# First attention of a fused four-layer kernel: sums over two groups at a time, and two projections split around a turn

## The chip, the cores and the metric

The kernel runs on one core of a Trainium2 chip, as one program. The metric is the device time of that core in microseconds, the median of several runs. Lower is better.

## What is computed

Two layers of a gated model, each an attention over a context followed by a feed-forward part, on 16 sequences of 112 tokens by 512 and a context of 375 tokens by 512. The change lies in the first attention alone:

```python
def _mha(q, k, v):                       # q = layernorm(x), k = v = ctx
    scores = jnp.einsum('bhqd,bhkd->bhqk', qh, kh) / math.sqrt(hd)   # 16 heads of 32
    scores = jnp.where(causal[None, None], scores, MASKED_BIAS)
    attn = jax.nn.softmax(scores, axis=-1)
    out = jnp.einsum('bhqk,bhkd->bhqd', attn, vh)
x = x + jnp.tanh(g_xattn[0]) * _L0_xattn_ref(_layernorm(x), ctx, ctx)
...
k = rms_norm((ctx @ Wk).reshape(B, S_enc, 4, 128))   # of the second attention
v = (ctx @ Wv).reshape(B, S_enc, 4, 128)
```

The phase of the first attention also computes the keys and values of the second attention, since it holds the transposed context, and turns and rotates weights and the first outputs for the feed-forward part that follows.

## The kernel before

`phase_a` works through 16 batches, each a sequence. A batch has 16 heads, taken as 8 pairs (n = 0 to 7) and as 4 groups of 4 heads (g = 0 to 3, pairs 2g and 2g+1). Each engine has its own hand-written program; they meet at semaphores, and each engine does its instructions in order. Nothing is scheduled by a planner: the order on TensorE is the sequence of `if n == ...` lines in the loop at the end of `phase_a`, and the loops of the other engines match it.

What TensorE does for a pair:

- at even n, `scores`: the scores of the next group of four heads (12 matmuls, line 910), which use 32 of the array's rows each;
- `turn_probs(b, n, 0)` (line 962): three transposes of the first head's probabilities into the PSUM bank `turned`. ScalarE copies them to `pT` (`probs_copy`, line 543). Then `turn_probs(b, n, 1)` does the second head into the same bank, so it waits for that copy (`pT_first`). VectorE copies the second (line 714), and the first turn of the next pair waits for it (`pT_second`);
- between the two turns and behind the second stands other work, to cover the copies. `weigh(b, g)` (line 972) is the weighted sum of group g: 12 matmuls of 32 columns of the array each, over three parts of the context, into the bank `outp`; the trace counts two matmuls and two weight loads for each. It stands between the turns of pairs 2, 4 and 6 (groups 0, 1 and 2) and of pair 0 of the next batch (group 3). ScalarE copies its block to `oT` (`copy_out`, line 570);
- `project` (line 939) makes keys or values of the second attention: 12 matmuls for each of three parts of the context, in two halves of 6. The other items are transposes of the context (`turn_ctx`, 889), the queries (896), the keys (`turn_keys`, 948), the output (`turn_back`, 980), weight jobs (989 to 1001), and from the third batch on the first output for the feed-forward part (`turn_z`, 1007, and `rotate_z`, 1014).

`outp` is one bank that many items use in turn. The list `out_uses` holds the order of its uses, and `free_out` waits for whoever reads the use before.

ScalarE at pair n: the copy of the first turn, `copy_out`, on some pairs `ctx_hi` or `rotated_hi` (line 593), then the exponentials of pair n+2 (line 535), then copies such as `values_out` (line 557) and `keys_out` (line 566). VectorE at pair n: at even n `maximum` of pair n+2 (lines 705 and 708), `scale_keys` (line 723) or `rotated_lo` (line 755), then the copy of the second turn, then at even n `maximum` of pair n+3. `scale_keys` waits for GpSimd's power (line 452). `turn_ctx(b + 1, 2)`, behind the first turn of pair 3, waits for `values_out(b, 0)`, because it writes the same bank.

`probs` has 4 slots of a pair each, `pT` two slots of a group each. The sync queue loads the context of batch b+2 (`load_ctx`) once `out_ready` says that the batch which held that buffer has been summed.

```python
                    if n in (2, 4, 6) and cur:
                        weigh(b, n // 2 - 1)
                    ...
                    if n == 2 and cur:
                        project(b, "v", 0, 1)
                    ...
                    if n == 6 and cur:
                        project(b, "k", 2, 1)
```

Of the kernel before, what the change touches and what calls it, by code (L numbers as in the profile page):

```python
# [30 lines left out]
HD = D // H  # L31
G = 4
# [86 lines left out]
CTX = 3  # L119
# [30 lines left out]
def phase_a(nc, keep, io, ab):  # L150
# [12 lines left out]
    RING = 4  # L163
# [3 lines left out]
    with Memory(nc, "a") as m:  # L167
# [10 lines left out]
        pT = m.sb("pT", [KP, 2, KC, HPG, S])  # L178
# [96 lines left out]
        def _(sp):  # L275
            def load_ctx(b):
# [9 lines left out]
                if b >= CTX:  # L286
                    sp.wait_ge(out_ready, G * (b - CTX) + G)
# [87 lines left out]
            def load_lead(c):  # L375

                sp.wait_ge(out_ready, G * (B - CTX + c) + G)
# [133 lines left out]
        def _(act):  # L511
# [16 lines left out]
            def exps(b, n):  # L528
# [4 lines left out]
                for i in range(2):  # L533
                    h = 2 * n + i
                    last = act.activation(probs[:, n % RING, i, 0:T], score[0:S, h % HPG, 0:T], ACT.Exp, bias=nmax[:, b % 2, h:h + 1],  # L535
                                          accum_out=sums[:, b % 2, h:h + 1])
                last.then_inc(probs_ready, 1)

            def probs_copy(b, n):

                act.wait_ge(turned_ready, 2 * (PAIRS * b + n) + 1)
                g, half = n // 2, n % 2
                act.activation(pT[:, g % 2, :, 2 * half, :], turned[0:KP, 0:KC * S].rearrange("p (c s) -> p c s", c=KC),  # L543
# [125 lines left out]
        def _(dve):  # L669
# [40 lines left out]
            def probs_copy(b, n):  # L710

                dve.wait_ge(turned_ready, 2 * (PAIRS * b + n) + 2)
                g, half = n // 2, n % 2
                dve.tensor_copy(pT[:, g % 2, :, 2 * half + 1, :], turned[0:KP, 0:KC * S].rearrange("p (c s) -> p c s", c=KC)).then_inc(pT_second, 1)
# [133 lines left out]
        def _(pe):  # L848
# [4 lines left out]
            def free_out(*use):  # L853
# [5 lines left out]
                if kind == "weigh":  # L859
                    pe.wait_ge(out_copied, G * b + i + 1)  # L860
# [53 lines left out]
            def project(b, what, c, half):  # L914
                bank, ready = (keys, k_ready) if what == "k" else (values, v_ready)
                cols = slice(0, D) if what == "k" else slice(D, 2 * D)
                if half == 0:
# [15 lines left out]
                for n, (s, r, k) in enumerate(passes):  # L933
                    if n // 6 == half:
# [6 lines left out]
                if half:  # L941
# [1778 lines left out]
```

## Time and profile before

| | |
|---|---|
| median of 3 runs | 2031.68 us (2031.16 to 2034.02) |
| the profiled execution, its own time | 2032.41 us |
| its span in the trace | 2030.7 us |
| mean granted clock of TensorE | 0.988 of 2.4 GHz |
| TensorE busy | 1964.1 us, 97% |
| its weight loads | 1629.0 us, 80% |
| VectorE, ScalarE, GpSimd busy | 61%, 57%, 42% |

The phase that the change touches is the first 585 us or so of the span. Times are from the start of the span. A row of the time line gives the start, the duration, the engine, the line, the operation, its output and inputs, the shape and how many were merged into the row; in brackets stands how long the engine was idle before it and what ended that. PE is TensorE's matmuls, PEld its weight loads, which run ahead of the matmuls. Matmuls are pipelined: one starts before the one before it has ended, so what a step costs is read from start to start, not from the durations.

### The profile page before, as it was taken

Reading aid. Unit: us, or ns where it says so; the run is one execution under the profiler, and the core shown is the slowest. Engines: PE = TensorE matmul, PEld = TensorE weight load, DVE = VectorE, ACT = ScalarE, POOL = GpSimd, SP = SyncE. Lnnn points to the kernel's source line nnn. Section 1 sums busy time; section 2 is a strip of 40 time slices with the busy share of each in tenths; the row PEclk is TensorE's granted clock in tenths of the full one; section 3 lists DMA queues with packets and bytes.
Section 4 is the critical chain, followed back from the end, with each engine's and each line's share of the span. In section 5 each row is a group of like instructions: output and inputs, shape, how many; then the busy total and the mean of one; then the engine's idle time right before and its main releaser. Section 6 shows DMA issues by size and latency. Waiting matters only on the chain. (4 is left out here: it accounts for less than half of the span.)

```text
span 2030.7 us, 37414 instructions
## 1 busy us (share of the span) xinstructions
PE 1964.1 (97%) x13369; PEld 1629.0 (80%) x13369; DVE 1237.1 (61%) x2272; ACT 1158.6 (57%) x3064; POOL 850.5 (42%) x1010
## 2 busy tenths in 40 slices
PE   7999999999999999999989997899999999989997
PEld 6777777777778888898868886799999999877875
DVE  7767666676645643564445555666666666466665
ACT  6666666666643333453333435877777777354554
POOL 3525536445434000000003444888888888122222
PEclk9999999999999999999999998999999999999999
DMA  5426346344364210203003335333333342421101
GB/s 188 158 95 194 127 129 214 120 160 138 109 224 170 88 63 1 73 1 120 1 26 104 117 113 160 92 86 115 111 102 100 108 117 87 125 64 51 33 29 38
DMA packets 195370, 210.67 MB, mean 104 GB/s; under 512 B 60912, under 2 KB 135712, under 8 KB 194688
## 3 DMA queue, kind: packets, MB, share of 16 engines
q1 hardware_dynamic: 195200, 208.43, 32.6%
q8 instruction: 104, 1.70, 0.4%
q14 instruction: 66, 0.54, 0.1%
HBM read 128.43 MB, written 79.95 MB: 103 GB/s over the span
## 5 line engine op out<-in xcount | busy, mean ns | idle before, releaser
L1883 POOL TENSOR_TENSOR qd_rows<-qd_rows,c_rsum 112x375 f32<-112x375 f32 x256 | 202.5, 812 | 79.1 <-DVE c_rsum L2013 72.7
L2019 DVE TENSOR_TENSOR c_pT_lo<-c_turned,c_pT_hi 128x336 fp32r<-128x336 f32 x256 | 128.4, 502 | 123.6 <-ACT c_pT_hi L1958 123.6
L1949 ACT ACTIVATE qd_rows<-c_score,c_nmax 112x375 f32<-112x375 f32 x256 | 146.9, 574 | 86.8 <-DVE c_nmax L2008 86.8
L1314 ACT ACTIVATE b_silu<-b_gate,ab_scales 128x512 f32<-128x512 f32 (+1 forms) x64 | 40.7, 637 | 253.8 <-PE b_up L1443 253.8
L1380 DVE SCALAR_TENSOR_TENSOR b_hidden<-b_up,ab_scales,b_silu 128x512 f32<-128x512 f32 (+1 forms) x64 | 43.7, 683 | 196.3 <-ACT b_silu L1314 196.3
L2313 POOL TENSOR_TENSOR f_probs<-f_probs,f_rsum 112x448 f32<-112x448 f32 x64 | 59.7, 933 | 206.6 <-DVE f_rsum L2437 206.6
L535 ACT ACTIVATE a_probs<-a_score,a_nmax 112x375 f32<-112x375 f32 x256 | 144.5, 575 | 3.0 <-DVE a_nmax L708 2.9
L2008 DVE TENSOR_REDUCE c_nmax<-c_score 112x1 f32<-112x375 f32 x256 | 137.7, 538 | 0.4 <-PE c_score L2090 0.4
L2352 ACT ACTIVATE f_probs<-f_score,f_nmax 112x112 f32<-112x112 f32 x256 | 86.5, 364 | 80.7 <-DVE f_nmax L2432 80.7
L1292 POOL TENSOR_TENSOR ab_zT<-ab_zT,keep_ln_eps 128x1 f32<-128x1 f32 x1 | 0.2, 190 | 298.7 <-DVE ab_zT L1414 298.7
L962 PE MATMUL a_turned<-keep_ident,a_probs 112*128 112x112 f32 x768 | 122.1, 268 | 1.9 <-ACT a_pT L543 1.0
L708 DVE TENSOR_REDUCE a_nmax<-a_score 112x2 f32<-112x750 f32 x128 | 120.1, 938 | 4.4
L962 PEld LDWEIGHTS a_turned<-keep_ident,a_probs 112*128 112x128 f32 x768 | 86.6, 142 | 40.0 <-issue 23.5
L1958 ACT ACTIVATE c_pT_hi<-c_turned 128x336 fp32r<-128x336 f32 x256 | 100.5, 445 | 26.7 <-PE c_turned L2101 26.7
L2101 PE MATMUL c_turned<-keep_ident,qd_rows 112*128 112x112 f32 x768 | 96.8, 260 | 10.9 <-DVE c_pT_lo L2019 8.6
L2101 PEld LDWEIGHTS c_turned<-keep_ident,qd_rows 112*128 112x128 f32 x768 | 84.9, 141 | 27.9 <-POOL qd_rows L1883 12.0
L705 DVE COPY_PREDICATED a_score<-keep_later,a_score 112x224 f32<-112x224 uint8 x128 | 49.9, 390 | 91.0 <-PE a_score L910 91.0
L2090 PE MATMUL c_score<-c_k_hi,c_q_hi 128*112 128x376 f32 x256 | 95.4, 373 | 5.7 <-DVE c_k_lo L2003 4.8
L1616 ACT ACTIVATE qd_rows<-q_q_bank 128x512 f32<-128x512 f32 x56 | 33.5, 598 | 114.0 <-PE q_q_bank L1725 114.0
L543 ACT ACTIVATE a_pT<-a_turned 128x336 f32<-128x336 f32 x128 | 57.6, 450 | 63.4 <-PE a_turned L962 62.3
L450 POOL TENSOR_TENSOR a_ssq_eps<-a_ssq,keep_rms_eps 128x4 f32<-128x4 f32 x48 | 9.6, 200 | 198.1 <-DVE a_ssq L718 198.1
L1457 PE MATMUL b_y<-b_wd_hi,b_hT_hi 128*128 128x512 f32 x224 | 87.6, 391 | 0.2 <-DVE b_hT_lo L1389 0.2
(354 smaller groups left out, 6025.8 us busy)
## 6 DMA issues: line engine op xcount, KB each, us to landing
q<-q_qT SPq DMA_DIRECT2D x14, 1024.0 KB, 5.7
qd_raws<-q SPq DMA_DIRECT2D x64, 224.0 KB, 3.0
v<-bq_raw SPq DMA_DIRECT2D x48, 256.0 KB, 2.1
qd_raws<-v SPq DMA_DIRECT2D x64, 192.0 KB, 2.8
k<-bq_raw SPq DMA_DIRECT2D x16, 752.0 KB, 4.0
qd_raws<-k SPq DMA_DIRECT2D x64, 188.0 KB, 2.4
wug<-a_ug_turned SPq DMA_DIRECT2D x32, 256.0 KB, 2.2
bq_raw<-in_ctx_dram SPq DMA_DIRECT2D x15, 512.0 KB
```

The costliest lines, as they stand in the source:

```text
L535: last = act.activation(probs[:, n % RING, i, 0:T], score[0:S, h % HPG, 0:T], ACT.Exp, bias=nmax[:, b % 2, h:h + 1], accum_out=sums[:, b % ...
L708: dve.tensor_reduce(nmax[:, b % 2, 2 * n:2 * n + 2], score[0:S, pair, 0:T], axis=AX.X, op=ALU.max, negate=True).then_inc(max_done, 1)
L962: last = pe.transpose(turned[0:KP, c * S:(c + 1) * S], probs[:, n % RING, i, c * KP:(c + 1) * KP], ident[0:S, 0:S])
L1457: last = pe.matmul(y[b][:, :], hT[s][:, p, b * P:(b + 1) * P], wd[r][:, p, :], start=c == 0 and k == 0, stop=c == IC - 1 and k == len(PASS ...
L1883: pool.tensor_tensor(probs[:, n % AHEAD, 0:T], probs[:, n % AHEAD, 0:T], rsum[:, n % (2 * H):n % (2 * H) + 1].broadcast_to([S, T]), ALU.mu ...
L1949: act.activation(probs[:, n % AHEAD, 0:T], score[n % AHEAD][0:S, 0:T], ACT.Exp, bias=nmax[:, c:c + 1], accum_out=sums[:, c:c + 1]).then_in ...
L1958: act.activation(pT[0][:, t % 2, :, j, :], src, ACT.Copy).then_inc(pT_hi, 1)
L2008: dve.tensor_reduce(nmax[:, c:c + 1], score[n % AHEAD][0:S, 0:T], axis=AX.X, op=ALU.max, negate=True).then_inc(max_done, 1)
L2019: dve.tensor_tensor(pT[1][:, t % 2, :, j, :], src, f32(pT[0][:, t % 2, :, j, :]), ALU.subtract).then_inc(pT_split, 1)
L2090: last = pe.matmul(score[n % AHEAD][0:S, 0:TE], q[s][:, t % RING, j, :], k[r][:, t % RING, :], start=i == 0, stop=i == len(PASSES) - 1)
L2101: last = pe.transpose(turned[n % 2][0:KP, c * S:(c + 1) * S], probs[:, n % AHEAD, c * KP:(c + 1) * KP], ident[0:S, 0:S])
L2352: last = act.activation(probs[:, t % RING, j, :], score[0:S, j, columns_of(t)], ACT.Exp, bias=nmax[:, t // 2 % 2, 2 * j + t % 2:2 * j + t ...
```

## The change

The weighted sums are done for two groups at a visit, 24 matmuls into two blocks of `outp`: groups 0 and 1 between the turns of pair 4, groups 2 and 3 between the turns of pair 0 of the next batch. Between the turns of pairs 2 and 6 stand now the first three of the six projection matmuls that used to follow the second turn; the other three follow it as before. ScalarE's copy takes both blocks, 224 columns, so two copies a batch in place of four. `pT` has three slots of a group, so that the groups of a visit stay until it is done; `probs` has three slots of a pair in place of four. The waits and the order of uses of `outp` follow.

```diff
-    RING = 4
+    RING, PT_RING, HALVES = 3, 3, G // 2
-        pT = m.sb("pT", [KP, 2, KC, HPG, S])
+        pT = m.sb("pT", [KP, PT_RING, KC, HPG, S])
...
-            out_uses += [("weigh", b - 1, G - 1), ("keys", b - 1, KC - 1), ("back", b - 1, 0)] if before else []
-            out_uses += [("job", b, 1), ("weigh", b, 0)] if cur else []
+            out_uses += [("weigh", b - 1, HALVES - 1), ("keys", b - 1, KC - 1), ("back", b - 1, 0)] if before else []
+            out_uses += [("job", b, 1)] if cur else []
             out_uses += [("ctx", b + 1, 1)] if after else []
-            out_uses += [("keys", b, 0), ("job", b, 3), ("weigh", b, 1)] if cur else []
+            out_uses += [("keys", b, 0), ("job", b, 3), ("weigh", b, 0)] if cur else []
...
-            out_uses += [("job", b, 5), ("weigh", b, 2), ("keys", b, 1), ("job", b, 7)] if cur else []
+            out_uses += [("job", b, 5), ("keys", b, 1), ("job", b, 7)] if cur else []
...
-                    sp.wait_ge(out_ready, G * (b - CTX) + G)
+                    sp.wait_ge(out_ready, HALVES * (b - CTX) + HALVES)
...
-            def copy_out(b, g):
-                act.wait_ge(out_ready, G * b + g + 1)
-                act.activation(oT[:, g, :], outp[:, 0:S], ACT.Copy).then_inc(out_copied, 1)
+            def copy_out(b, m):
+                act.wait_ge(out_ready, HALVES * b + m + 1)
+                act.activation(oT[:, 2 * m:2 * m + 2, :], outp[:, 0:2 * S].rearrange("p (g s) -> p g s", g=2), ACT.Copy).then_inc(out_copied, 1)
...
-                        copy_out(b - 1, G - 1)
-                    if n in (2, 4, 6) and cur:
-                        copy_out(b, n // 2 - 1)
+                        copy_out(b - 1, HALVES - 1)
+                    if n == 4 and cur:
+                        copy_out(b, 0)
...
-            def project(b, what, c, half):
+            def project(b, what, c, first, end):
...
-                    if n // 6 == half:
+                    if first <= n < end:
...
-            def weigh(b, g):
-                pe.wait_ge(pT_first, PAIRS * b + 2 * g + 2)
-                pe.wait_ge(pT_second, PAIRS * b + 2 * g + 2)
-                free_out("weigh", b, g)
-                for c in range(KC):
-                    for j in range(HPG):
-                        h = HPG * g + j
-                        last = pe.matmul(outp[rows(j), 0:S], ctx[:, b % CTX, c, h * HD:(h + 1) * HD], pT[:, g % 2, c, j, :],
-                                         start=c == 0, stop=c == KC - 1)
+            def weigh(b, m):
+
+                pe.wait_ge(pT_first, PAIRS * b + 4 * m + 4)
+                pe.wait_ge(pT_second, PAIRS * b + 4 * m + 4)
+                free_out("weigh", b, m)
+                for i in range(2):
+                    g = 2 * m + i
+                    for c in range(KC):
+                        for j in range(HPG):
+                            h = HPG * g + j
+                            last = pe.matmul(outp[rows(j), i * S:(i + 1) * S], ctx[:, b % CTX, c, h * HD:(h + 1) * HD],
+                                             pT[:, (G * b + g) % PT_RING, c, j, :], start=c == 0, stop=c == KC - 1)
                 last.then_inc(out_ready, 1)
...
-                        weigh(b - 1, G - 1)
+                        weigh(b - 1, HALVES - 1)
...
-                    if n in (2, 4, 6) and cur:
-                        weigh(b, n // 2 - 1)
+                    if n == 2 and cur:
+                        project(b, "v", 0, 6, 9)
+                    if n == 4 and cur:
+                        weigh(b, 0)
+                    if n == 6 and cur:
+                        project(b, "k", 2, 6, 9)
...
                     if n == 2 and cur:
-                        project(b, "v", 0, 1)
+                        project(b, "v", 0, 9, 12)
...
                     if n == 6 and cur:
-                        project(b, "k", 2, 1)
+                        project(b, "k", 2, 9, 12)
```

TensorE's order at pair 2 of a batch in the middle, from the first turn on, before (a_outp<-a_pT is weigh, a_values is the projection, a_outp<-keep_ident,bq_raw is turn_ctx of part 1, the last row turn_ctx of part 2):

```order
L962 MATMUL a_turned<-keep_ident,a_probs 128x112 x3
L972 MATMUL a_outp<-a_pT,bq_raw 32x112 x12
L962 MATMUL a_turned<-keep_ident,a_probs 128x112 x3
L939 MATMUL a_values<-a_w_lo,a_kT_hi 128x512 x2
L939 MATMUL a_values<-a_w_hi,a_kT_lo 128x512 x4
L889 MATMUL a_outp<-keep_ident,bq_raw 128x128 x4
L962 MATMUL a_turned<-keep_ident,a_probs 128x112 x3
L889 MATMUL a_values<-keep_ident,bq_raw 128x128 x4
```

and now:

```order
L962 MATMUL a_turned<-keep_ident,a_probs 128x112 x3
L939 MATMUL a_values<-a_w_lo,a_kT_hi 128x512 x2
L939 MATMUL a_values<-a_w_hi,a_kT_lo 128x512
L962 MATMUL a_turned<-keep_ident,a_probs 128x112 x3
L939 MATMUL a_values<-a_w_hi,a_kT_lo 128x512 x3
L889 MATMUL a_outp<-keep_ident,bq_raw 128x128 x4
L962 MATMUL a_turned<-keep_ident,a_probs 128x112 x3
L889 MATMUL a_values<-keep_ident,bq_raw 128x128 x4
```

The 12 matmuls of weigh are gone from between the two turns, and three of the six projection matmuls stand there.

TensorE's order at pair 6 of the same batch, before (a_values<-ab_zT is rotate_z, a_keys the projection, a_outp<-keep_ident,a_kn is turn_keys of part 1, and the last row but one is the first turn of pair 7):

```order
L962 MATMUL a_turned<-keep_ident,a_probs 128x112 x3
L972 MATMUL a_outp<-a_pT,bq_raw 32x112 x12
L1014 MATMUL a_values<-ab_zT,keep_hadamard 128x448
L962 MATMUL a_turned<-keep_ident,a_probs 128x112 x3
L939 MATMUL a_keys<-a_w_lo,a_kT_hi 128x512 x2
L939 MATMUL a_keys<-a_w_hi,a_kT_lo 128x512 x4
L948 MATMUL a_outp<-keep_ident,a_kn 128x128 x4
L962 MATMUL a_turned<-keep_ident,a_probs 128x112 x3
```

and now:

```order
L962 MATMUL a_turned<-keep_ident,a_probs 128x112 x3
L939 MATMUL a_keys<-a_w_lo,a_kT_hi 128x512 x2
L939 MATMUL a_keys<-a_w_hi,a_kT_lo 128x512
L1017 MATMUL a_values<-ab_zT,keep_hadamard 128x448
L962 MATMUL a_turned<-keep_ident,a_probs 128x112 x3
L939 MATMUL a_keys<-a_w_hi,a_kT_lo 128x512 x3
L948 MATMUL a_outp<-keep_ident,a_kn 128x128 x4
L962 MATMUL a_turned<-keep_ident,a_probs 128x112 x3
```

Again three projection matmuls take the place of weigh; rotate_z stays between the turns, behind them.

TensorE's order at pair 4, before (a_outp<-keep_ident,a_xn is the transposes of the queries):

```order
L962 MATMUL a_turned<-keep_ident,a_probs 128x112 x3
L972 MATMUL a_outp<-a_pT,bq_raw 32x112 x12
L962 MATMUL a_turned<-keep_ident,a_probs 128x112 x3
L939 MATMUL a_values<-a_w_hi,a_kT_hi 128x512 x4
L939 MATMUL a_values<-a_w_lo,a_kT_hi 128x512 x2
L896 MATMUL a_outp<-keep_ident,a_xn 128x112 x4
```

and now:

```order
L962 MATMUL a_turned<-keep_ident,a_probs 128x112 x3
L975 MATMUL a_outp<-a_pT,bq_raw 32x112 x24
L962 MATMUL a_turned<-keep_ident,a_probs 128x112 x3
L939 MATMUL a_values<-a_w_hi,a_kT_hi 128x512 x4
L939 MATMUL a_values<-a_w_lo,a_kT_hi 128x512 x2
L896 MATMUL a_outp<-keep_ident,a_xn 128x112 x4
```

The visit has 24 matmuls in place of 12. At pair 0 it grows in the same way.

## Rows read from the trace of the kernel before

**Rows 1.** 40 to 560 us: length, then busy us of PE, PEld, DVE, ACT, POOL, PEclk, DMA.

```profile
40.00:560.00 520.00, 519.20 (x4653) 403.26 (x4651) 354.93 (x629) 351.73 (x928) 250.40 (x274) 1.00 0.44 143
```

**Rows 2.** Time line: TensorE at pair 2 of batch 8; start, duration, then what it is.

```profile
308.32 0.51 PE L962 MATMUL a_turned<-keep_ident,a_probs 112*128 112x112 f32 x3
...
308.75 0.54 PEld L972 LDWEIGHTS a_outp<-a_pT,bq_raw 128*32 128x32 f32 x24
...
309.47 0.51 PE L962 MATMUL a_turned<-keep_ident,a_probs 112*128 112x112 f32 x3
...
309.74 0.71 PE L939 MATMUL a_values<-a_w_lo,a_kT_hi 128*128 128x512 f32 x2
...
310.29 1.09 PE L939 MATMUL a_values<-a_w_hi,a_kT_lo 128*128 128x512 f32 x4
...
311.22 0.60 PE L889 MATMUL a_outp<-keep_ident,bq_raw 128*128 128x128 f32 x4
...
311.65 0.45 PE L962 MATMUL a_turned<-keep_ident,a_probs 112*128 112x112 f32 x3
...
312.16 0.63 PE L889 MATMUL a_values<-keep_ident,bq_raw 128*128 128x128 f32 x4
```

**Rows 3.** Time line: ScalarE and VectorE at the same pair 2.

```profile
308.86 0.45 ACT L543 ACTIVATE a_pT<-a_turned 128x336 f32<-128x336 f32 x1 [1.94 <-PE a_turned L962]
...
310.03 0.69 DVE L723 TENSOR_TENSOR a_kn<-a_keys,a_rk 128x512 f32<-128x512 f32 x1 [0.22 <-POOL a_rk L452]
...
310.64 0.50 DVE L714 COPY a_pT<-a_turned 128x336 f32<-128x336 f32 x1
310.86 0.20 ACT L535 ACTIVATION_READ_ACCUMULATOR a_probs<-a_score,a_nmax 112x1 f32 x1
...
311.42 0.60 ACT L557 ACTIVATE bq_raw<-a_values 128x512 f32<-128x512 f32 x1 [0.36 <-PE a_values L939]
```

**Rows 4.** Time line: TensorE at pair 6 of batch 8.

```profile
325.69 0.51 PE L962 MATMUL a_turned<-keep_ident,a_probs 112*128 112x112 f32 x3
...
326.84 1.02 PE L1014 MATMUL a_values<-ab_zT,keep_hadamard 128*128 128x448 f32 x2
...
327.69 0.45 PE L962 MATMUL a_turned<-keep_ident,a_probs 112*128 112x112 f32 x3
...
327.92 0.71 PE L939 MATMUL a_keys<-a_w_lo,a_kT_hi 128*128 128x512 f32 x2
...
329.82 0.45 PE L962 MATMUL a_turned<-keep_ident,a_probs 112*128 112x112 f32 x3
```

**Rows 5.** Time line: ScalarE and VectorE at the same pair 6.

```profile
327.89 0.55 ACT L593 ACTIVATE ab_xr_hi<-a_values 128x448 fp32r<-128x448 f32 x1 [0.66 <-PE a_values L1014]
...
328.47 0.62 DVE L755 SCALAR_TENSOR_TENSOR ab_xr_lo<-a_values,ab_xr_hi 128x448 fp32r<-128x448 f32 x1 [1.29 <-ACT ab_xr_hi L593]
...
329.01 0.50 DVE L714 COPY a_pT<-a_turned 128x336 f32<-128x336 f32 x1
```

**Rows 6.** Time line: pair 6 of batch 1, which has no rotation.

```profile
78.57 0.51 PE L962 MATMUL a_turned<-keep_ident,a_probs 112*128 112x112 f32 x3
...
80.27 0.51 DVE L714 COPY a_pT<-a_turned 128x336 f32<-128x336 f32 x1 [0.21 <-PE a_turned L962]
```

**Rows 7.** Groups by line and form: weigh's weight loads, and the copy of its block.

```profile
L972 PEld LDWEIGHTS a_outp<-a_pT,bq_raw 128*32 128x32 f32 x1536 | 34.6, 109 | 9.8 <-issue 1.0
...
L570 ACT ACTIVATE a_oT<-a_outp 128x112 f32<-128x112 f32 x64 | 16.8, 263 | 18.9 <-PE a_outp L972 18.7
```

**Rows 8.** Time line: TensorE at pair 0 of batch 9, weigh and turn_keys.

```profile
334.89 0.78 PE L972 MATMUL a_outp<-a_pT,bq_raw 128*32 128x112 f32 x24
...
336.38 0.60 PE L948 MATMUL a_outp<-keep_ident,a_kn 128*128 128x128 f32 x4
```

**Rows 9.** Time line: a turn of pair 7, batch 15, released by ScalarE's copy.

```profile
577.07 0.44 ACT L543 ACTIVATE a_pT<-a_turned 128x336 f32<-128x336 f32 x1
...
577.57 0.51 PE L962 MATMUL a_turned<-keep_ident,a_probs 112*128 112x112 f32 x3 [0.37 <-ACT a_pT L543]
```

More of the change, by code:

```diff
@@ L534, in exps @@
                     h = 2 * n + i
-                    last = act.activation(probs[:, n % RING, i, 0:T], score[0:S, h % HPG, 0:T], ACT.Exp, bias=nmax[:, b % 2, h:h + 1],
+                    last = act.activation(probs[:, t % RING, i, 0:T], score[0:S, h % HPG, 0:T], ACT.Exp, bias=nmax[:, b % 2, h:h + 1],
                                           accum_out=sums[:, b % 2, h:h + 1])
@@ L541, in probs_copy @@
                 act.wait_ge(turned_ready, 2 * (PAIRS * b + n) + 1)
-                g, half = n // 2, n % 2
-                act.activation(pT[:, g % 2, :, 2 * half, :], turned[0:KP, 0:KC * S].rearrange("p (c s) -> p c s", c=KC),
+                k, half = divmod(PAIRS * b + n, 2)
+                act.activation(pT[:, k % PT_RING, :, 2 * half, :], turned[0:KP, 0:KC * S].rearrange("p (c s) -> p c s", c=KC),
                                ACT.Copy).then_inc(pT_first, 1)
@@ L712, in probs_copy @@
                 dve.wait_ge(turned_ready, 2 * (PAIRS * b + n) + 2)
-                g, half = n // 2, n % 2
-                dve.tensor_copy(pT[:, g % 2, :, 2 * half + 1, :], turned[0:KP, 0:KC * S].rearrange("p (c s) -> p c s", c=KC)).then_inc(pT_second, 1)
+                k, half = divmod(PAIRS * b + n, 2)
+                dve.tensor_copy(pT[:, k % PT_RING, :, 2 * half + 1, :], turned[0:KP, 0:KC * S].rearrange("p (c s) -> p c s", c=KC)).then_inc(pT_second, 1)
             def sum_keys(b, c):
@@ L912, in scores @@
                 last.then_inc(scores_ready, 1)
-            def project(b, what, c, half):
+            def project(b, what, c, first, end):
                 bank, ready = (keys, k_ready) if what == "k" else (values, v_ready)
                 cols = slice(0, D) if what == "k" else slice(D, 2 * D)
-                if half == 0:
+                if first == 0:
                     if what == "v" and c == 2 and b >= 2:
@@ L940, in project @@
                                          start=n == 0, stop=n == len(passes) - 1)
-                if half:
+                if end == len(passes):
                     last.then_inc(ready, 1)
@@ L961, in turn_probs @@
                 for c in range(KC):
-                    last = pe.transpose(turned[0:KP, c * S:(c + 1) * S], probs[:, n % RING, i, c * KP:(c + 1) * KP], ident[0:S, 0:S])
+                    last = pe.transpose(turned[0:KP, c * S:(c + 1) * S], probs[:, t % RING, i, c * KP:(c + 1) * KP], ident[0:S, 0:S])
                 last.then_inc(turned_ready, 1)
-            def weigh(b, g):
-                pe.wait_ge(pT_first, PAIRS * b + 2 * g + 2)
-                pe.wait_ge(pT_second, PAIRS * b + 2 * g + 2)
-                free_out("weigh", b, g)
-                for c in range(KC):
-                    for j in range(HPG):
-                        h = HPG * g + j
-                        last = pe.matmul(outp[rows(j), 0:S], ctx[:, b % CTX, c, h * HD:(h + 1) * HD], pT[:, g % 2, c, j, :],
-                                         start=c == 0, stop=c == KC - 1)
+            def weigh(b, m):
[9 more added lines that the diff above has]
+                                             pT[:, (G * b + g) % PT_RING, c, j, :], start=c == 0, stop=c == KC - 1)
                 last.then_inc(out_ready, 1)
             def turn_back(b):
-                pe.wait_ge(out_copied, G * b + G)
+                pe.wait_ge(out_copied, HALVES * b + HALVES)
                 free_out("back", b, 0)
@@ L1019, in _ @@
             scores(0, 0)
-            project(0, "k", 0, 0)
+            project(0, "k", 0, 0, 6)
             for b in range(B + 1):
@@ L1086, in _ @@
                         run_job(b, 7)
-                        project(b, "v", 2, 1)
+                        project(b, "v", 2, 6, 12)
 IC = INTER // P
```

22 lines of the change are left out of this document (11 added, 11 removed).

## The prediction

> **What bounds the kernel now.** I read the summary page first: TensorE is busy for 97% of the span. The table of stretches then shows that in the middle of the first attention, from 40 to 560 us, it is busy for 519.20 of 520 us at a granted clock of 1.00, while VectorE and ScalarE are at 355 and 352 us [rows 1]. The view of waits lists no wait of TensorE's matmuls there. So in this phase TensorE's own chain of starts is the time, and an edit is worth what it changes between two starts on TensorE. The other engines matter only where a release comes later than TensorE would arrive. I therefore read the time line around the two pairs that change, in one batch; the 16 batches repeat it within 0.02 us, but for the first two and the last.
>
> I count from T, the start of the first turn of a pair. Pair 2 of batch 8 has T = 308.32 [rows 2]: weigh starts at T+0.43, the second turn at T+1.15, the projection (6 matmuls) at T+1.42, turn_ctx at T+2.90, pair 3's first turn at T+3.33 and its turn_ctx at T+3.84. Pair 6 has T = 325.69 [rows 4]: rotate_z at T+1.15, the second turn at T+2.00, pair 7's first turn at T+4.13.
>
> **What a visit costs.** From weigh's start to the next is 0.72 us, and reaching it takes 0.43 after T, against 0.27 for a projection behind a turn (309.47 to 309.74) [rows 2]. A visit issues 24 weight loads of 109 ns [rows 7], and all 24 lie within 0.54 us [rows 2]: (0.54 - 0.11)/23 = 0.0187 us from one to the next. Twelve more matmuls, thus 24 more loads in the same mode, cost 24 x 0.0187 = 0.45 us. This length isn't in the trace of before. Its bounds are 0.45 (the rate of the row goes on) and 0.72 (the second group pays a whole visit). I take 0.45, since nothing stands between the groups and the operands have the same shape. The Trainium skill speaks against it: "TensorE: Matmul & The Clock Gate", part 3 on packing small matmuls, says that a weight load overlaps running matmuls only where the row group differs, and these loads fill all rows. By that rule the 24 loads would be serial, 24 x 0.109 = 2.6 us in place of 0.45. The row shows them overlapped, so I keep 0.45.
>
> **Added:** pairs 4 and 0 get the longer visit: 16 + 16 visits x 0.45 = **+14.4 us**. It lies on TensorE's chain, with nothing beside it. The last of these, behind the last batch, delays the end of the phase by the same 0.45.
>
> **Removed at pair 2 (16 times).** If TensorE were never held up: three projection matmuls start at T+0.27; two take 0.55 (309.74 to 310.29) and one 0.23 (a quarter of 310.29 to 311.22), so the second turn would be at T+1.05. It waits for ScalarE's copy, which ends at T+0.99 [rows 3]; with a release of 0.06 to 0.14 (below) that is T+1.05 to T+1.13, a loss under 0.1 that what follows hides. Then 0.23 to the projection (327.69 to 327.92 [rows 4]), 0.78 for three matmuls (the first behind a turn is dearer), 0.43 for turn_ctx: pair 3 would begin at T+2.49, 0.84 earlier than now. **Two releases don't allow that.** VectorE copies pair 2's second probabilities behind maximum and scale_keys. scale_keys starts at T+1.71, where GpSimd's a_rk releases it, and the copy ends at T+2.82 [rows 3]. All of that hangs on work of pair 1 or on the scores, which start no earlier relative to T, so it stays. And turn_ctx of part 2 waits for values_out: ScalarE ends its exponentials at T+2.74, needs 0.60 for the copy, so it can end at T+3.37 (now T+3.70) [rows 3]. A release takes 0.14 us from the end of the copy to the start of the matmul where two conditions are waited for (312.02 to 312.16) [rows 2, 3] and 0.06 where there is one (577.51 to 577.57) [rows 9]. I take 0.14, as both places have two. So pair 3 begins at T+2.96 and its turn_ctx at T+3.51, against T+3.84: a gain of 0.33, x 16 = **-5.3 us**.
>
> **Removed at pair 6.** Without holds: rotate_z at T+0.27+0.78 = T+1.05, second turn 0.85 later, then 0.23 + 0.78 + 0.44, so pair 7 at T+3.35. But its first turn waits for a chain that begins at rotate_z: ScalarE's rotated_hi (T+2.20), VectorE's rotated_lo (T+2.78), then its copy of the probabilities, which ends at T+3.82 [rows 5]. rotate_z comes only 0.10 earlier, so the copy ends at T+3.72 and pair 7 begins at T+3.86 to T+3.87, against T+4.13: a gain of 0.26 where 0.78 were there to take; x 13 (batches 2 to 14) = **-3.4 us**. The first two batches have no rotation: their copy ends at T+2.21 [rows 6], ahead of need at T+2.49, and I give them pair 2's free gain of 0.84 to 0.85. The last batch computes no keys for a next one and has slack around this pair; I give it the same: 3 x 0.85 = **-2.6 us**.
>
> **Costed at nothing.** The block's copy grows from 112 to 224 columns: 263 ns now [rows 7], 450 for 336 columns [rows 3], so about 0.36 by line. At pair 0 it must end before turn_keys(2), which starts 1.49 us behind weigh now [rows 8] and 1.94 in the new order; the block is ready at 0.78 + 0.45 = 1.23, its copy at some 1.66, released by 1.80. The cover is 0.14 us; if it is gone, each 0.1 us lost costs 1.6 us. RING of 3 adds no wait: the slot asked for was turned before the copy that precedes the exponentials on ScalarE. The third pT buffer is written behind a turn that itself stands behind the visit that read it. On the sync queue, load_ctx and what is queued behind it go at most 0.45 later; its data are due a batch later. DVE's and POOL's orders are unchanged.
>
> **Sum:** +14.4 - 5.3 - 3.4 - 2.6 = **+3.1 us**. The profiled execution took 2032.41 us (span 2030.7), 0.73 above the median of the three runs, so it becomes 2035.5 and the median 2031.68 becomes **2034.8 us**. One measurement of this kernel tells 0.2% from no change, which is 4.06 us: 2027.6 to 2035.7. My number is inside, near the upper edge.
>
> **Rivals.**
> *A, the holds are not there, faster.* If VectorE's and ScalarE's chains move forward with TensorE, the gains are 16 x 0.84 + 13 x 0.78 + 3 x 0.85 = 26.1 us against 14.4: -11.7, thus 2020.0. For it: both engines idle almost a third of the phase. Against it: the rows put the two copies at T+2.82 and T+3.82, behind work that starts from T. Chance 0.09.
> *B, the second group isn't free of entry and exit, slower.* The mechanism is in weigh itself: if the array empties between the two groups, as between a turn and a visit, the visit grows by 0.72 and not by 0.45: 32 x 0.27 = 8.6 more, +11.7, thus 2043.4. It would decide from 0.03 us more a visit (0.9/32), since my sum is 0.9 below the edge. For it: every change of kind around weigh costs 0.16 to 0.18 us. Against it: inside a visit three accumulations of four matmuls follow each other with no gap in the loads. Chance 0.10.
> *C, serial weight loads.* If loads that fill all rows couldn't overlap, the second group would cost 2.6 us: 32 x (2.6 - 0.45) = 69 more, thus 2104. The row of 24 loads in 0.54 us speaks against it. Chance 0.01. This is the rule of the Trainium skill's TensorE page, part 3, quoted above.
>
> **How the numbers follow.** The forecast has the remaining 0.80. Its own bounds: with releases of 0.06 the two gains grow by 0.08 each, 29 x 0.08 = 2.3 lower, 2032.5; a reading error of 0.03 us at each of 61 places is 1.8 either way, a loss of 0.1 at the tight copy of pair 0 adds 1.6, and the first two batches and the last, taken by analogy, are good for 1.7 either way. That is 2029 to 2040, the range, with A, B and C outside (0.20). Of the 0.80, 0.02 lie below 2027.6, 0.50 within 0.2%, and 0.28 above 2035.7. So faster 0.09 + 0.02 = 0.11, same 0.50, slower 0.28 + 0.10 + 0.01 = 0.39.
>
> **What would show it.** In the profile after: weigh with 48 loads in about 1.0 us, and 1.16 to 1.17 to the next start; pair 2's first turn to pair 3's first turn 2.96 us, with a wait on pT of VectorE of some 0.4 us, 16 times; pair 6 to pair 7 3.87 us with such a wait of 0.5 us, 13 times; a batch longer by 0.9 - 0.33 - 0.26 = 0.3 us. I am wrong if VectorE's copy stops being the release of these turns (A), if the loads show a gap between the 24th and the 25th (B), or if turn_keys at pair 0 begins to wait for the block's copy.

## The result, and the profile after

The changed kernel's median is 2033.67 us over 20 runs (2031.34 to 2037.84), that of the kernel before beside it 2031.54 us over 20 runs. The ratio is 1.0013, with a 95% interval from 1.0007 to 1.0019: slower by 2.6 us (1.4 to 3.9), which is clear of zero and within the 0.2% that I called no change. The forecast was 3.1 us more. The profiled execution took 2032.96 us, its span is 2031.2.

The stretch of [rows 1], for the kernel after (the columns are length, then busy us of PE, PEld, DVE, ACT, POOL, PEclk, DMA share, GB/s):

```profile
40.00:560.00 520.00, 511.39 (x4606) 397.29 (x4604) 352.04 (x625) 339.96 (x889) 247.99 (x272) 1.00 0.44 143
```

TensorE is no longer busy all the time, 511.39 us of 520 against 519.20. What took the rest is named by the view of waits, 40 to 560 us, matmuls of TensorE (total us, times, longest):

```profile
PE a_turned L962 <- ACT a_probs L535: 4.6, 13, 0.4
PE a_turned L962 <- DVE a_pT L714: 3.6, 14, 0.3
```

The kernel before had no row here. There are now 27 waits: at pair 3 in 14 batches and at pair 7 in 13, those in the window. The name ACT a_probs on the second kind is misleading: the turn waits for two conditions, and the view names the one whose signal it saw last. The experiment on pair 6 shows that it is VectorE's copy: with that copy earlier, the turn starts at T+3.26 while the same ScalarE row still runs to T+3.67. No other wait of TensorE's matmuls stands in this view, so the ring of three slots, the third buffer of `pT` and the later loads of the context, which the prediction put at nothing, held no matmul here.

Pair 2 of batch 8 in the time line, answering [rows 2, 3]:

```profile
308.11 0.51 PE L962 MATMUL a_turned<-keep_ident,a_probs 112*128 112x112 f32 x3
...
310.42 0.50 DVE L714 COPY a_pT<-a_turned 128x336 f32<-128x336 f32 x1
310.65 0.20 ACT L535 ACTIVATION_READ_ACCUMULATOR a_probs<-a_score,a_nmax 112x1 f32 x1
310.74 0.60 ACT L557 ACTIVATE bq_raw<-a_values 128x512 f32<-128x512 f32 x1
...
311.07 0.48 PE L962 MATMUL a_turned<-keep_ident,a_probs 112*128 112x112 f32 x3 [0.26 <-DVE a_pT L714]
...
311.48 0.63 PE L889 MATMUL a_values<-keep_ident,bq_raw 128*128 128x128 f32 x4
```

With T = 308.11 VectorE's copy ends at T+2.81, pair 3 begins at T+2.96 and its turn_ctx at T+3.37 (before: T+2.82, T+3.33, T+3.84). The second turn starts at 309.16, T+1.05. Those but the last are the forecast to 0.01 us; turn_ctx is 0.14 earlier than forecast.

Pair 6 of batch 8, answering [rows 4, 5]:

```profile
325.57 0.51 PE L962 MATMUL a_turned<-keep_ident,a_probs 112*128 112x112 f32 x3
...
326.63 0.91 PE L1017 MATMUL a_values<-ab_zT,keep_hadamard 128*128 128x448 f32 x2
...
327.58 0.54 ACT L593 ACTIVATE ab_xr_hi<-a_values 128x448 fp32r<-128x448 f32 x1 [1.01 <-PE a_values L1017]
...
328.16 0.62 DVE L755 SCALAR_TENSOR_TENSOR ab_xr_lo<-a_values,ab_xr_hi 128x448 fp32r<-128x448 f32 x1 [1.10 <-ACT ab_xr_hi L593]
...
328.70 0.50 DVE L714 COPY a_pT<-a_turned 128x336 f32<-128x336 f32 x1
...
329.34 0.48 PE L962 MATMUL a_turned<-keep_ident,a_probs 112*128 112x112 f32 x3 [0.36 <-ACT a_probs L535]
```

With T = 325.57: rotate_z at T+1.06, rotated_hi T+2.01, rotated_lo T+2.59, VectorE's copy ends T+3.63, pair 7 begins T+3.77 (before T+4.13, forecast T+3.86). rotate_z behind a projection takes 0.75 us to the next start, not the 0.85 that it took behind weigh, and the chain moves forward by that.

The visit, at pair 4 of batch 8, with its weight loads:

```profile
316.69 0.51 PE L962 MATMUL a_turned<-keep_ident,a_probs 112*128 112x112 f32 x3
...
317.13 1.12 PEld L975 LDWEIGHTS a_outp<-a_pT,bq_raw 128*32 128x32 f32 x48
...
318.42 0.51 PE L962 MATMUL a_turned<-keep_ident,a_probs 112*128 112x112 f32 x3
```

From weigh to the next start it is 1.29 us, not the 1.17 of the forecast. The reason is in the rate. The stretches count every load that overlaps a slice of 0.1 us; a load lasts 0.11, so it counts about twice. Before (batch 8, pair 2), loads of line 972 alone:

```profile
308.80:308.90 0.10, 0.10 (x12) 1.00 0.85 307
...
309.00:309.10 0.10, 0.10 (x9) 1.00 0.78 287
```

After (pair 4), loads of line 975:

```profile
317.20:317.30 0.10, 0.10 (x12) 1.00 0.00 0
317.30:317.40 0.10, 0.10 (x8) 1.00 0.00 0
...
318.00:318.10 0.10, 0.10 (x8) 1.00 0.94 369
```

The first eight come close together (12 in a slice), then it is 8 in every slice. By the starts of the single loads in the trace, the first eight lie within 0.05 us and from then on four follow every 0.096 us, in both kernels: 0.024 us a load. The 25th starts 0.077 us behind the 24th, as the first of every four does, so there is no gap between the two groups. My 0.0187 was the mean over a visit that had the dense beginning in it. Twelve more matmuls, 24 loads, cost 24 x 0.024 = 0.58 us. The matmuls keep the same step, four every 0.096 us, so the trace doesn't say whether the loads or the matmuls set it.

The block's copy took 357 ns for 224 columns (forecast 0.36), by the groups of lines.

Batch 8 to batch 9, from pair 2's first turn to the next pair 2's, is 35.25 us after (308.11 to 343.36) and was 34.95: +0.30 a batch, with +0.31 forecast. (Some batches take longer, up to 35.8 us before; from the third on each grows by 0.3 to 0.4.)

**Why the two spans differ by 0.5 us only.** The spans are 2030.7 and 2031.2, and yet the phase has grown by more. The profiled executions start differently. The stretch from 17 to 27 us, of the kernel before, of the kernel after, and of the kernel after in another execution (the first experiment below):

```profile
17.00:27.00 10.00, 8.48 (x44) 6.41 (x40) 8.25 (x14) 6.17 (x15) 0.41 (x2) 0.66 0.85 261
```

```profile
17.00:27.00 10.00, 7.78 (x54) 5.74 (x55) 9.16 (x16) 5.97 (x16) 1.88 (x4) 1.00 0.86 253
```

```profile
17.00:27.00 10.00, 8.16 (x52) 6.30 (x49) 8.36 (x15) 5.86 (x15) 1.14 (x4) 0.83 0.86 262
```

The granted clock (the number before the last two) is 0.66, 1.00 and 0.83 of 2.4 GHz there, the last two for the same code: where the mean is under 1.00, TensorE ran at the lower level, 1.2 GHz, for part of the stretch. In all three it had waited before, for the first copies of the probabilities (0.58 us at 18 us, 0.9 to 1.3 us at 20 us); the execution that stayed at 1.00 waited no less, so what decides stays open. The kernel before reached pair 2 of batch 0 at 27.52 us, the one after at 25.49: 2.0 us that are no work of the change. From there to the first matmul of the next phase it is 558.41 and 562.01 us (which starts at 585.93 and 587.50). So in these two executions the phase grew by 3.6 us, and in the other execution of the kernel after it is 562.05 us again. The remaining 1.0 us lies behind the phase, whose code is the same: 1444.8 us before, 1443.7 after, and 1442.1 in the other execution of the kernel after. The timed runs give 1.4 to 3.9 for the change.

### The profile page after: what moved, and what is told of

Read it like the earlier page. It is cut to its first block and busy times, and to the rows that moved or that the text cites. A ratio compares the mean times of both kernels' runs of the same rounds, so it can differ in the third digit from the quotient of the medians.

```text
span 2031.2 us, 37351 instructions
## 1 busy us (share of the span) xinstructions
PE 1958.2 (96%) x13369; PEld 1624.6 (80%) x13369; DVE 1236.8 (61%) x2272; ACT 1149.7 (57%) x3032; POOL 850.6 (42%) x1010
## 5 line engine op out<-in xcount | busy, mean ns | idle before, releaser
L962 PEld LDWEIGHTS a_turned<-keep_ident,a_probs 112*128 112x128 f32 x768 | 84.4, 141 | 56.6 <-issue 27.5
L2131 PE MATMUL c_y<-o_wo_hi,c_oT_lo 128*128 128x512 f32 x224 | 87.7, 391 | 0.0
```

The source lines that it names most:

```text
L962: last = pe.transpose(turned[0:KP, c * S:(c + 1) * S], probs[:, t % RING, i, c * KP:(c + 1) * KP], ident[0:S, 0:S])
L2131: last = pe.matmul(y[:, :], oT[s][:, h, place], wo[r][:, h, :], start=h == 0 and n == 0, stop=h == H - 1 and n == len(PASSES) - 1)
```

## Experiments

Nine other kernels ran after the prediction, and the changed one once more, in three groups, each on a chip of its own beside the kernel before. Ratios are to that kernel, with their 95% intervals; between groups the ratios are compared, not the medians. Numbers behind T are from their traces, batch 8 unless said.

The traces give a second measure, which leaves out the start and everything behind the phase: from pair 2 of batch 0 to the first matmul of the next phase. The two executions of the changed kernel agree in it to 0.03 us, while the rest of the span, behind the phase, lies anywhere from 1442.1 to 1447.4 us in the twelve profiled executions. For each kernel, what differs from the kernel before (558.41 us in this measure; in brackets the name that the quoted expectations use):

| kernel | phase, by its trace | timed runs (from the ratio) |
|---|---|---|
| the change | +3.6 us | +2.6 us (+1.4 to +3.9) |
| the change once more | +3.6 | +2.6 (+0.8 to +4.5) |
| pair 6 (a_dve6) | -3.1 | -5.9 (-8.1 to -3.7) |
| pair 2 (a_dve2) | +3.5 | +2.8 (+1.0 to +4.5) |
| pair 2 again (a_dve2_pe3) | +2.9 | +1.6 (-0.2 to +3.5) |
| both (a_all) | -4.4 | -4.5 (-6.5 to -2.4) |
| both, and context part 2 later (a_all2) | -11.6 | -12.4 (-15.2 to -9.5) |
| the five moves in the kernel before | -3.5 | -3.0 (-4.9 to -1.2) |
| VectorE's two orders in the kernel before | +0.2 | +1.6 (-0.2 to +3.5) |
| visits issued twice | +36.7 | +36.2 (+33.1 to +39.0) |
| projections whole again | +3.9 | +4.1 (+1.8 to +6.3) |

The two measures agree within the intervals, but for pair 6, where the trace gives 0.6 us less than the edge; why isn't shown.

### The changed kernel once more

No edit.

> The changed kernel itself, beside the others on this chip: 0.07 to 0.19% above the kernel before, a batch 0.30 us longer in its trace. If instead it is level or faster, the slower result was the chip's and not the kernel's.

Measured: 1.0013 (1.0004 to 1.0022), median 2033.62. The result stands in a second measurement.

### Pair 6: VectorE's copy ahead of rotated_lo

```diff
-                    if n == 6 and b >= 2 and cur:
-                        rotated_lo(b - 2)
                     if n == 7 and cur:
                         sum_keys(b, 2)
                     if cur:
                         probs_copy(b, n)
+                    if n == 6 and b >= 2 and cur:
+                        rotated_lo(b - 2)
```

> The changed kernel, with VectorE's copy of pair 6's probabilities ahead of rotated_lo. Theory (VectorE's copy, queued behind rotated_lo, holds pair 7's first turn): the copy ends at T+2.8, so that turn comes at T+3.35 in place of T+3.77, in 13 batches: 5.5 us less than the changed kernel, about 2028.2, which is 0.16% below the kernel before. The projection of pair 7 waits for rotated_lo, due at T+3.57 as before, so no new wait. Rival (another release stands right behind, for instance rotated_lo itself for that projection): nothing gained, 2033.7.

Measured: 0.9971 (0.9960 to 0.9982), median 2025.98. Against the changed kernel's 1.0013 that is 0.42% or 8.5 us less; the batch went from 35.25 to 34.73 us (306.38 to 341.11), which over 13 batches is 6.8; the phase is 6.7 us shorter in its trace. The forecast of 5.5 was too low, and the 8.5 of the timed runs has room for 6.7 in its interval. Its pair 6:

```profile
323.83 0.51 PE L962 MATMUL a_turned<-keep_ident,a_probs 112*128 112x112 f32 x3
...
326.13 0.51 DVE L714 COPY a_pT<-a_turned 128x336 f32<-128x336 f32 x1 [0.81 <-PE a_turned L962]
...
326.55 0.61 DVE L755 SCALAR_TENSOR_TENSOR ab_xr_lo<-a_values,ab_xr_hi 128x448 fp32r<-128x448 f32 x1
...
327.09 0.45 PE L962 MATMUL a_turned<-keep_ident,a_probs 112*128 112x112 f32 x3
```

The copy ends at T+2.81 and pair 7 begins at T+3.26, with no wait. The next row of the chain, rotated_lo, ends at T+3.33 and held nobody. So the wait was VectorE's copy behind rotated_lo, and moving one line of one queue turns the change from slower into faster than the kernel before. The expected T+3.35 was 0.09 too late, for the shorter rotate_z.

### Pair 2: VectorE's copy ahead of scale_keys

```diff
-                    if n == 2 and cur:
-                        scale_keys(b, 0)
...
                     if cur:
                         probs_copy(b, n)
+                    if n == 2 and cur:
+                        scale_keys(b, 0)
```

> The changed kernel, with VectorE's copy of pair 2's probabilities ahead of scale_keys. Theory (two releases hold pair 3, and the later one is ScalarE's values_out for turn_ctx): pair 3's first turn moves from T+2.96 to T+2.50, but turn_ctx of part 2 stays at T+3.37, so the time stays within 1 us of 2033.7. Rival (VectorE's copy alone is the hold): 16 x 0.46 = 7.4 us less, 2026.3.

Measured: 1.0014 (1.0005 to 1.0022), median 2033.54, as the changed kernel; the phase is 0.1 us shorter. Its pair 2:

```profile
309.13 0.51 PE L962 MATMUL a_turned<-keep_ident,a_probs 112*128 112x112 f32 x3
...
311.67 0.45 PE L962 MATMUL a_turned<-keep_ident,a_probs 112*128 112x112 f32 x3
...
311.76 0.59 ACT L557 ACTIVATE bq_raw<-a_values 128x512 f32<-128x512 f32 x1
...
312.50 0.63 PE L889 MATMUL a_values<-keep_ident,bq_raw 128*128 128x128 f32 x4 [0.38 <-ACT bq_raw L557]
```

Pair 3 begins at T+2.54 in place of T+2.96, and turn_ctx at T+3.37 as before, now with 0.38 us of waiting for values_out. The wait that the view of waits shows at pair 3 was real and worth nothing: another one ended later. The rival is out.

### Pair 2 again, with pair 3's projection ahead of turn_ctx

The edit above, and on TensorE:

```diff
-                    if n == 3 and after:
-                        turn_ctx(b + 1, 2)
                     if n == 3 and cur:
                         project(b, "k", 1, 0, 6)
+                    if n == 3 and after:
+                        turn_ctx(b + 1, 2)
```

> As a_dve2, and on TensorE the first half of pair 3's projection stands ahead of turn_ctx of part 2. Theory: the projection waits only for scale_keys (release at T+2.91), turn_ctx comes at T+4.4, long after values_out, and pair 3's second turn at T+4.76 in place of T+5.22: 15 x 0.46 = 6.9 us less than the changed kernel, 2026.8. Rival (ScalarE's and VectorE's copies of that context part come 1 us later and hold the scores of pair 4 instead): no gain.

Measured: 1.0008 (0.9999 to 1.0017), median 2032.73. The gain of 0.34% is not there; the phase is 0.7 us shorter, where 6.9 were expected. Pair 3's second turn does come at T+4.69 (expected T+4.76), but it is given back before pair 4. Its view of waits, 40 to 560 us:

```profile
PE a_outp L992 <- ACT bq_raw L566: 1.8, 7, 0.3
PE a_outp L1004 <- ACT bq_raw L566: 1.8, 7, 0.3
```

Both rows are new: the job of pair 3 (of either kind), in 14 batches; in the one of batch 8 the weight loads stand still for 0.69 us. The rival had the right kind of cause (the copies of context part 2 come later) and the wrong place.

### Both

> Both holds taken away: pair 6 as in a_dve6 and pair 2 as in a_dve2_pe3. Theory: the two gains add up, 5.5 + 6.9 = 12.4 us less than the changed kernel, 2021.3, and 0.5% below the kernel before. Rival: the second gain is lost to the next wait and it stays at one of them, 2027 to 2028.

Measured: 0.9978 (0.9968 to 0.9988), median 2026.98. By the timed runs it can't be told from pair 6 alone (0.9971), by the traces it is 1.2 us better: the rival, nearly, and far from the 6.9 more of the theory. What happens at pair 3 (pair 2's T = 304.46):

```profile
309.35 0.60 ACT L521 ACTIVATE a_kT_hi<-a_values 128x512 fp32r<-128x512 f32 x1 [0.83 <-PE a_values L889]
...
309.84 0.57 ACT L535 ACTIVATE a_probs<-a_score,a_nmax 112x375 f32<-112x375 f32 x1
...
310.94 0.70 ACT L566 ACTIVATE bq_raw<-a_outp,keep_qk_w 128x512 f32<-128x512 f32 x1
...
311.68 0.66 PE L992 MATMUL a_outp<-keep_ident,a_ug_raw 128*128 128x128 f32 x4 [0.25 <-ACT bq_raw L566]
```

ScalarE can do ctx_hi of part 2 only at 309.35, since turn_ctx now comes later; behind it in its queue stand pair 5's exponentials and keys_out, which ends at 311.64, and job 3 on TensorE writes the bank that keys_out reads. From pair 2 to pair 4 it takes 8.51 us, against 8.58 in the changed kernel.

### Both, and context part 2 later on ScalarE and VectorE

On top of the kernel above:

```diff
 ScalarE
-                    if n == 3 and after:
-                        ctx_hi(b + 1, 2)
...
                     if n == 3 and cur:
                         keys_out(b, 0)
+                    if n == 3 and after:
+                        ctx_hi(b + 1, 2)
 VectorE
-                    if n == 3 and after:
-                        ctx_lo(b + 1, 2)
...
                     if cur:
                         probs_copy(b, n)
...
+                    if n == 3 and after:
+                        ctx_lo(b + 1, 2)
```

> a_all, and the copies of context part 2 stand later: on ScalarE ctx_hi behind the exponentials and keys_out of pair 3, on VectorE ctx_lo behind its copy of the probabilities. Theory (in a_all job 3 waited for keys_out, which stood behind the late ctx_hi on ScalarE, and took back the 0.5 us gained at pair 3): the wait on keys_out goes, and 15 x 0.45 = 6.8 us come off a_all, about 0.55% below the kernel before. Rival (the next wait, for the scores or for the projection of pair 4, stands right behind): as a_all, 0.2 to 0.3% below the kernel before.

Measured: 0.9939 (0.9925 to 0.9953), median 2019.32 us (2018.23 to 2020.18). It is the best of all kernels here, 12.4 us below the kernel before and 15 below the change. The same place in its time line:

```profile
300.86 0.51 PE L962 MATMUL a_turned<-keep_ident,a_probs 112*128 112x112 f32 x3
...
306.46 0.69 ACT L566 ACTIVATE bq_raw<-a_outp,keep_qk_w 128x512 f32<-128x512 f32 x1 [0.38 <-PE a_outp L948]
...
307.67 0.60 PE L992 MATMUL a_outp<-keep_ident,a_ug_raw 128*128 128x128 f32 x4
...
308.90 0.51 PE L962 MATMUL a_turned<-keep_ident,a_probs 112*128 112x112 f32 x3
```

keys_out ends at 307.15, the job starts at 307.67 without a wait, and pair 4 begins 8.04 us behind pair 2. A batch takes 34.19 us (300.86 to 335.05), 0.76 less than before; the whole phase is 11.6 us shorter. No wait of a matmul is left in its view of waits.

### Control: the same five moves in the kernel before

> Control of a_all2: the same five moves (VectorE's copies of pairs 2 and 6 forward, pair 3's projection ahead of turn_ctx, ctx_hi and ctx_lo of part 2 later) in the kernel before, visits and projections as they were. Theory (the moves take away holds that mostly came with the change; the kernel before has only one, turn_ctx behind values_out, 0.22 us): 15 x 0.22 = 3.3 us less, 0.16% below the kernel before, with pairs 3 and 7 beginning at T+3.33 and T+4.13 as before; so the change itself is worth the other 0.45% of a_all2 once its holds are gone. Rival (the moves help by themselves, whatever the visits): about 2019, as a_all2.

Measured: 0.9985 (0.9976 to 0.9994), median 2028.24. In its time line:

```profile
304.52 0.51 PE L962 MATMUL a_turned<-keep_ident,a_probs 112*128 112x112 f32 x3
...
307.86 0.45 PE L962 MATMUL a_turned<-keep_ident,a_probs 112*128 112x112 f32 x3
...
309.55 0.60 PE L889 MATMUL a_values<-keep_ident,bq_raw 128*128 128x128 f32 x4
```

Pair 3 begins at T+3.34 as before; its projection is the next start, 0.22 later, and turn_ctx no longer waits. So the moves alone are worth 0.15%. The other 0.46% of the best kernel need the change: by the traces 3.5 us and 8.1 us of the 11.6.

### Control: VectorE's two orders in the kernel before

> Control: the kernel before, with VectorE's two orders of a_dve6 and a_dve2 (its copy ahead of rotated_lo at pair 6 and of scale_keys at pair 2). Theory (in the kernel before these copies are ready in time, so the holds came with the change): pair 7's and pair 3's first turns stay at T+4.13 and T+3.33, same time within 1 us. Rival (the order on VectorE was a cost of its own already): faster by up to the 5 to 8 us that it gave the changed kernel.

Measured: 1.0008 (0.9999 to 1.0017). The interval includes 1, though by the medians it is 2.3 us, more than the 1 us expected. The trace has no such loss: its pair 2,

```profile
307.28 0.51 PE L962 MATMUL a_turned<-keep_ident,a_probs 112*128 112x112 f32 x3
...
308.98 0.51 DVE L714 COPY a_pT<-a_turned 128x336 f32<-128x336 f32 x1 [0.21 <-PE a_turned L962]
...
310.62 0.45 PE L962 MATMUL a_turned<-keep_ident,a_probs 112*128 112x112 f32 x3
```

begins pair 3 at T+3.34, its turn_ctx comes at T+3.84, and the batch takes 34.91 us. VectorE's copy ends 0.62 us earlier and TensorE doesn't notice; the whole phase differs by 0.2 us. So the rival, 5 to 8 us faster, is out. Whether the two orders cost something small that the trace doesn't show stays open.

### The kernel before, each visit's twelve matmuls issued twice

```diff
-                for c in range(KC):
+                for c in (*range(KC), *range(KC)):
                     for j in range(HPG):
```

> The kernel before, with the twelve matmuls of each visit issued twice in a row into the same block (the sums are started afresh, so the second dozen gives the same result as the first): 64 visits of 24 instead of 12. Theory (behind the first loads a visit runs at 4 loads in 0.097 us): 24 more loads cost 0.58 us each, 64 x 0.58 = 37 us, and a visit takes 1.29 to 1.30 to the next start. Rival (the first visit's mean of 18.7 ns a load goes on, and the longer visit of the change has another cause, such as the second block or the third buffer): 64 x 0.45 = 29 us and 1.17.

Measured: 1.0178 (1.0163 to 1.0192), 36.2 us more (33.1 to 39.0) where 37 were expected, and 29 by the rival. A visit at pair 2:

```profile
327.37 1.11 PEld L972 LDWEIGHTS a_outp<-a_pT,bq_raw 128*32 128x32 f32 x48
...
328.66 0.51 PE L962 MATMUL a_turned<-keep_ident,a_probs 112*128 112x112 f32 x3
```

48 loads in 1.11 us, and 1.29 to the next start, the same as in the changed kernel with one block and two buffers. So the 0.58 is the rate of such pairs of loads and matmuls, and comes neither from the second block nor from the third buffer. Putting the two groups in another order inside the visit was not tried.

### The changed kernel with both projections whole again

```diff
-                    if n == 2 and cur:
-                        project(b, "v", 0, 6, 9)
...
-                    if n == 6 and cur:
-                        project(b, "k", 2, 6, 9)
...
-                        project(b, "v", 0, 9, 12)
+                        project(b, "v", 0, 6, 12)
...
-                        project(b, "k", 2, 9, 12)
+                        project(b, "k", 2, 6, 12)
```

> The changed kernel, with both split projections whole again behind the second turn. Theory: at pair 2 nothing is lost before the second turn (ScalarE's copy releases it at T+1.05 either way), then the projection is 0.78 longer, of which 0.46 were a wait anyway; pair 3's turn_ctx at T+3.5 against T+3.37. At pair 6 rotate_z comes 0.8 earlier, and with it the chain that holds pair 7, which starts at T+3.25 in place of T+3.77. 15 x 0.15 more, 13 x 0.5 less: about 4 us less than the changed kernel, 2029.4. Rival (the three projection matmuls are the needed cover between the turns): 32 x 0.3 to 0.8 more, 2043 to 2059.

Measured: 1.0020 (1.0009 to 1.0031), median 2034.15; expected was 0.9990. The rival (2043 or more) is out by far, but the gain isn't there. Half of the theory held. Pair 6:

```profile
327.24 0.51 PE L962 MATMUL a_turned<-keep_ident,a_probs 112*128 112x112 f32 x3
...
327.58 0.93 PE L1017 MATMUL a_values<-ab_zT,keep_hadamard 128*128 128x448 f32 x2
...
330.48 0.45 PE L962 MATMUL a_turned<-keep_ident,a_probs 112*128 112x112 f32 x3
```

rotate_z covers ScalarE's copy, the chain is early, and pair 7 begins at T+3.24. Pair 2, with T = 309.39:

```profile
310.44 0.51 PE L962 MATMUL a_turned<-keep_ident,a_probs 112*128 112x112 f32 x3 [0.54 <-ACT a_pT L543]
...
312.40 0.60 ACT L557 ACTIVATE bq_raw<-a_values 128x512 f32<-128x512 f32 x1 [0.26 <-PE a_values L939]
...
313.14 0.63 PE L889 MATMUL a_values<-keep_ident,bq_raw 128*128 128x128 f32 x4
```

TensorE stands still for 0.54 us before the second turn, and turn_ctx comes at T+3.75, not T+3.5: I had kept values_out at its old time, but it reads what the projection writes, and the projection is 0.78 later now. The split is worth 0.38 us a batch at pair 2, and costs 0.53 at pair 6, where rotate_z stands between the turns anyway. A batch in the middle is 35.08 us, 0.17 shorter than in the changed kernel. The expectation also left out the first two batches: without rotate_z nothing else covers ScalarE's copy at pair 6, pair 7 begins at T+3.23 in place of T+2.55, and each of them is 1.08 us longer (34.89 against 33.81). That uses up the gain: over the 15 batches the two kernels differ by less than 0.1 us, and over the phase by 0.3. The split at pair 2 alone, with pair 6 whole from the third batch on, wasn't run.

## Why the prediction was right, term by term

The direction, the size and the two holds came out as forecast. That the sum is so close is in part luck: the visits were costed 4.0 us too low, the gains at pairs 2 and 6 3.3 us too low, and these errors cancel for the most part.

- **The longer visit**, forecast 0.45 (+14.4 us over 32), measured 0.575 (1.29 and 0.72 at pairs 4 and 0): +18.4 us. This is the term with the largest error. I had named bounds of 0.45 and 0.72 and took the lower; the trace of before allowed a better reading, since its loads in slices already thin out behind the first ones (x12, then x9).
- **Pair 2**, forecast 0.33, measured 0.47 (turn_ctx at T+3.37 and not T+3.51): 15 x 0.47 = -7.1 us, and 0.25 in the last batch. That the end of values_out decides there was right (the first experiment on pair 2 shows it). What was off is its start. The exponentials end at T+2.74 in both kernels, and I let the copy start 0.03 behind that; when its input is ready, ScalarE starts it 0.11 before the end of the row ahead (310.74 against 310.65 + 0.20), so it ends at T+3.23 and not T+3.37. Rows of before show the same overlap: the row at 310.86 [rows 3] starts 0.11 before the end of the one ahead, and I didn't use it.

```profile
310.40 0.57 ACT L535 ACTIVATE a_probs<-a_score,a_nmax 112x375 f32<-112x375 f32 x1
```

- **Pair 6**, forecast 0.26, measured 0.36: 13 x 0.36 = -4.7 us. The chain was right link by link; rotate_z took 0.10 less to the next start behind a projection.
- **The first two batches and the last**, forecast 3 x 0.85: 0.79 twice (3.34 to 2.55), and 0.94 in the last (575.34 - 570.69 = 4.65 before, 577.02 - 573.31 = 3.71 after; there weigh had waited 0.49 us for ScalarE's copy of a job before, and now VectorE's copy holds pair 7 for 0.35): -2.5 us.
- **The end of the phase**, not in the forecast: at pair 7 of the last batch the second turn waited 0.37 us for ScalarE's copy before [rows 9] and doesn't now, which gives 0.50 us; turn_keys behind the last visit waits 0.38 us for the copy of the block, where it waited 0.29 before (+0.09); and the stand before the next phase's first matmul is 2.03 us in place of 2.30. Together -0.7 us.
- **Sum by the traces:** 18.4 - 7.1 - 0.2 - 4.7 - 2.5 - 0.7 = +3.2 us, where the two executions differ by 3.6 from pair 2 of batch 0 to the next phase (the 0.4 between them is 0.02 to 0.03 us a batch, the grain of the readings), and the timed runs say 2.6 (1.4 to 3.9).
- **Costed at nothing:** the block's copy before turn_keys at pair 0 held in its 0.14 us of cover in the middle of the phase (turn_keys at T+2.51 of pair 0, 0.29 behind the turn, as before). Behind the last batch it adds the 0.09 us named above.
- **Rival A** (no holds) was wrong as a statement on the changed kernel, and its price was about right for the kernel in which the holds are really gone: -11.7 forecast, -12.4 measured (-11.6 by the trace). That agreement is luck in part: 3 of it come from a hold that the kernel before has too, and the visits cost 4 more than this price allowed. **Rival B** (a whole visit for the second group) would have been 0.72; half of the way there was real, by a steady rate and not by an entry and exit. **Rival C** (serial loads): 24 loads cost 0.58 us, not 2.6. The rule of the Trainium skill ("TensorE: Matmul & The Clock Gate", part 3), that loads overlap only with matmuls of other row groups, is not what these loads show: they fill all 128 rows, use 32 columns each, about four and a half of them are under way at any time (0.11/0.024), and they run beside the visit's matmuls (48 loads in the 1.12 us from 317.13, 48 matmul records in the 1.36 us from the same start).

## What to carry to other kernels

Where one engine is busy all the time, work taken from it is worth only what the queues behind it can follow: ask for each start that would come earlier which release it waits for, and what stands in front of the releasing instruction on its own engine. Removing a wait that the view of waits shows, here 3.6 us in all, may give nothing while a second one ends later; five short moves, four in other queues (the copy that TensorE waits for first, the copy that has time last) and one on TensorE, turned a change of +0.13% into one of -0.61%, of which they give 0.15% without the change. A rate for a longer burst is read from the steady part of a short one, not from its mean.

## What the runs showed of the hardware

- Pairs of a weight load of 32 columns over all rows and a matmul of 112 columns, one behind the other in four column groups, run at four in 0.096 us once the first eight loads are out, at a granted clock of 1.00; 24 of them more cost 0.58 us in a visit, shown by two kernels. Whether loads or matmuls set the step isn't shown.
- In these kernels the hadamard matmul of 448 columns takes 0.75 us to the next start behind a projection and 0.85 behind the 32-column matmuls.
- In the first 30 us the granted clock differs between executions of the same code (0.83 and 1.00 from 17 to 27 us for the changed kernel, and 0.66 in the kernel before, which gives TensorE the same work up to there). Over the twelve profiled executions pair 2 of batch 0 begins at 25.5 to 25.9 us where that mean is 1.00, at 26.4 to 26.8 where it is 0.83, and at 27.5 to 27.6 where it is 0.66. Of the 2.0 us between the two executions above, 0.3 are there by the first scores at 11 us, ahead of this stretch; the other 1.7 is more than half of what the change costs.
